# GpSimd's bias additions, the value projection's banks and the first scores moved; second biases gathered by expert number

## The reference

```python
x = x + gnn(layernorm(x), gW1, gb1, gW2, gb2)        # two graph convolutions over 10000 edges + self loops
# ffn of layernorm(x), 625 rows of 768:
h = ln(x, ln1_g, ln1_b); q, k, v = h @ Wq, h @ Wk, h @ Wv          # 12 heads of 64
x = x + softmax(causal(q k^T) * 768**-0.5) v @ Wp + bp
h2 = ln(x, ln2_g, ln2_b)
w, sel = top_k(h2 @ Wg, 1); w = softmax(w)           # one of 8 experts for each row
y = relu(h2 @ W1[e] + b1[e]) @ W2[e] + b2[e]         # 768 -> 3072 -> 768, for the chosen expert e
out = x_in + x + w * y                               # the outer residual too
```

## Time and profile before

| | us |
|---|---|
| median of 3 runs | 882.34 |
| lowest, highest | 880.31, 886.64 |
| the profiled execution: time | 882.35 |
| the profiled execution: span | 880.8 |
| busy in it: PE, DVE, ACT, POOL | 846.6, 713.1, 552.9, 78.3 |
| share of the clock granted to TensorE over the span | 0.993 |

### The profile page before, as it was taken

How to read it: one execution, slowest core, us unless ns; L and a number is a source line. 1 busy time by engine, 2 the same in 40 slices (tenths; PEclk the granted TensorE clock), 3 DMA queues, 4 the chain that set the end, 5 groups by cost and what they waited for, 6 DMA issues and landing times.

```text
span 880.8 us, 14635 instructions
## 1 busy us (share of the span) xinstructions
PE 846.6 (96%) x5326; PEld 815.4 (93%) x5326; DVE 713.1 (81%) x1102; ACT 552.9 (63%) x785; POOL 78.3 (9%) x85
## 2 busy tenths in 40 slices
PE   7999999989899998999989999999999999999997
PEld 7989999989789888898989999999999999999996
DVE  6999586873578787755788897998989899898996
ACT  4612341352577777614577877888878888787880
POOL 2000000230400000031600000000000000000041
PEclk9999999999999999999999999999999999999998
DMA  7030017162930033430799999999999999999984
GB/s 219 22 108 1 19 25 156 53 161 67 319 116 2 1 108 92 159 89 1 251 361 355 355 338 377 346 364 373 351 377 359 364 373 351 376 347 374 373 279 139
DMA packets 116232, 196.00 MB, mean 223 GB/s; under 512 B 34052, under 2 KB 83420, under 8 KB 116182
## 3 DMA queue, kind: packets, MB, share of 16 engines
q1 hardware_dynamic: 107858, 168.88, 56.4%
q0 software_dynamic: 6368, 24.19, 8.0%
q10 hardware_dynamic: 1956, 2.26, 1.0%
HBM read 177.40 MB, written 17.90 MB: 222 GB/s over the span
## 4 chain that ended last, share of the span: by engine, by line
PE 61%; DVE 19%; DMA 11%; issue 4%; ACT 4%; SPq 0%; DVEq 0%; ACTq 0%
PE ps L1502 12%; PE ps L1905 11%; DMA raw<-in_L_ffn_W 11%; PE ps L1924 10%; DVE wlo L1002 10%; PE ps L1686 7%; PE ps L1531 4%; PE ps L1757 3%; PE ps L1735 2%; PE ps L1582 2%; PE ps L1608 2%; PE ps L1720 2%; PE ps L1890 2%; ACT whi L668 2%; DVE ohs L1054 1%
## 5 line engine op out<-in xcount | busy, mean ns | idle before, releaser
L1002 DVE TENSOR_TENSOR wlo<-raw,whi 128x2304 fp32r<-128x2304 f32 (+1 forms) x150 | 352.7, 2359 | 22.8 <-ACT whi L668 22.4
L668 ACT ACTIVATE whi<-raw 128x2304 fp32r<-128x2304 f32 (+1 forms) x152 | 300.7, 1980 | 80.9 <-DMA raw<-in_L_ffn_W 33.7
L1924 PE MATMUL ps<-whi,hTT 128*128 128x384 f32 x768 | 201.5, 339 | 0.7 <-ACT oh7T L668 0.7
L1924 PEld LDWEIGHTS ps<-whi,hTT 128*128 128x128 f32 x768 | 139.1, 188 | 1.0 <-ACT oh7T L668 1.0
L1905 PE MATMUL ps<-whi,hgh 128*128 128x384 f32 x384 | 133.0, 346 | 1.0 <-DVE hgl L1002 1.0
L1924 PE MATMUL ps<-wlo,hTT 128*128 128x384 f32 x384 | 129.0, 336 | 0.0
L1905 PE MATMUL ps<-whi,hgl 128*128 128x384 f32 x384 | 129.0, 336 | 0.0
L1905 PE MATMUL ps<-wlo,hgh 128*128 128x384 f32 x384 | 128.4, 334 | 0.0
L1905 PEld LDWEIGHTS ps<-whi,hgh 128*128 128x128 f32 x384 | 72.2, 188 | 1.2 <-DVE hgl L1002 1.2
L1924 PEld LDWEIGHTS ps<-wlo,hTT 128*128 128x128 f32 x384 | 72.3, 188 | 0.0
L1905 PEld LDWEIGHTS ps<-wlo,hgh 128*128 128x128 f32 x384 | 72.3, 188 | 0.0
(11 more groups left out here) (294 smaller groups left out, 1589.2 us busy)
## 6 DMA issues: line engine op xcount, KB each, us to landing
raw<-in_L_ffn_W SPq DMA_DIRECT2D x128, 1152.0 KB, 6.9
hs_d<-bc POOLq DMA_DIRECT2D x13, 384.0 KB, 6.4
raw<-in_L_gnn_W SPq DMA_DIRECT2D x4, 1152.0 KB, 5.8
hs<-hs_d POOLq DMA_DIRECT2D x8, 384.0 KB, 5.6
ys_d<-ysb POOLq DMA_DIRECT2D x7, 384.0 KB, 5.9
raw<-in_L_ffn_Wv SPq DMA_DIRECT2D x6, 384.0 KB, 5.2
raw<-in_L_ffn_Wq SPq DMA_DIRECT2D x12, 192.0 KB, 3.6
raw<-in_L_ffn_Wk SPq DMA_DIRECT2D x12, 192.0 KB, 3.5
```

The source lines that it names most:

```text
L668: act.activation(out_, in_, func).then_inc(s, 1)
L1002: dve.tensor_tensor(out_, in_, hi_, ALU.subtract).then_inc(s, 1)
L1924: ins = mm(ps[0:CAP, 4 + half, 0:HB], l, rr, start=k == 0 and j == 0 and jj == 0, stop=k == FCH - 1 and j == JW - 1 and jj == 2)
```

## The change

It has seven parts.

1. **Graph part.** `P1_BANK` goes from (6, 0, 2, 6, 4) to (6, 6, 2, 6, 4), and `transform(1)` waits for `h0_out(0)` (s_hev 1) in place of all three `counts`; `transform(3)` waits for s_hev 2.
2. **Bias additions on POOL.** The third addition waits for the low part of Wv's second half (s_flo 6), the fourth and fifth for hTl chunks 2 and 4 (s_hTl).
3. **Value projection.** Its banks are 6 - 2(c%2) in place of 4 + 2(c%2); chunk 0 waits for four of the five `s_x1`, chunk 1 for the fifth.
4. **First scores.** The order of the first products is g = 0, 2, 1, then `scores(0)`, then g = 3; g = 1 goes to bank 6. ACT and DVE follow (`qk_out(3)` behind the first exponents and maxima).
5. **First weight chunk.** `split_hi(0, 0)` and `split_lo(0, 0)` are made in two halves; DVE's first half stands ahead of its wait for the gates, the second where the whole stood.
6. **Pick.** CHOICE_BUSY goes from 12 to 9, blocks lie in banks 6, 7, 5 by pairs (`picked`), and ACT starts on each of the first two pairs when it is there.
7. **Second biases.** oh8T, its five transposes, b2's hi and lo and all `bias_y` products go. Instead POOL, behind the first `next_in`, gathers b2's rows by `eidx` into `x2` (five indirect DMAs), and DVE adds them times wtok to `base` in steps 9 to 13 of the first tile. Y_BACK_AT goes from 10 to 8, and the fifth `others_y` moves ahead of the low parts of y.

```diff
 LAST_BANK = (0, 2, 6, 4, 0)
+QK_FIRST = (0, 2, 1, 3)
 FIN_ORDER = ((0, 0), (1, 0), (2, 0), (0, 1), (1, 1), (2, 1), (3, 0), (3, 1), (4, 0), (4, 1))
-Y_BACK_AT = 10
+Y_BACK_AT = 8
+B2_AT = 9
 OVER_N2 = 5
...
 FIRST_COUNTS_AT = 67
-P1_BANK = (6, 0, 2, 6, 4)
+P1_BANK = (6, 6, 2, 6, 4)
 PR = P + 2
...
 SHORT = 2
-TURN_BUSY, GATE_BUSY, RANK_BUSY, CHOICE_BUSY = 3, 3, 8, 12
+TURN_BUSY, GATE_BUSY, RANK_BUSY, CHOICE_BUSY = 3, 3, 8, 9
 EARLY = 4
...
+
+        def picked(m):
+
+            return ps[0:128, (6, 7, 5)[m // 2], m % 2 * 128:m % 2 * 128 + CAP]
...
-            return ps[:, 6 if g >= 4 else g, 0:HALF]
+            return ps[:, g if g in (0, 2, 3) else 6, 0:HALF]
...
+
+        def qk_count(g):
+
+            return C + (QK_FIRST.index(g) if g < 4 else g) + 1
...
                 g.wait_ge(s_n1, c + 1)
+                if c == 2:
+                    g.wait_ge(*split(2 * WV + 2))
+                elif c >= 3:
+                    g.wait_ge(s_hTl, 2 * c - 4)
                 gp.tensor_tensor(xf[:, c, :], xf[:, c, :], bc[1][0:P, :], ALU.add).then_inc(s_xfb, 1)
...
                 g.dma_start(tok(xf_d)[r0:r1, :, :], xf[r0:r1, :, :]).then_inc(s_xfst, 16)
-            g.dma_start(bc[1][0:E, :], b2[:, :]).then_inc(s_b2in, 16)
...
             next_in(0)
+            g.wait_ge(s_base, C)
+            for c in range(C):
+                g.indirect_dma_start(out=x2[:, c, :], out_offset=None, in_=b2[:, :],
+                                     in_offset=bass.IndirectOffsetOnAxis(ap=eidx[:, c:c + 1], axis=0)
+                                     ).then_inc(s_b2in, 16)
             with g.Fori(1, E) as t:
...
                 y_out(t)
-            g.wait_ge(s_base, C)
+            g.wait_ge(s_b2, C)
             g.wait_ge(s_route, 1)
...
                 if held:
-                    a.wait_ge(s_pj, C + 2 * held[-1] + 2)
+                    a.wait_ge(s_pj, C + max(2 * held[-1] + 2, 4))
                 else:
...
-                a.wait_ge(s_pj, C + g + 1)
+                a.wait_ge(s_pj, qk_count(g))
                 if not g:
...
             a.wait_ge(s_x2, C)
-            split_hi(0, 0)
+            a.wait_ge(s_raw[0], FULL[0] + 16)
+            act.activation(whi[0][:, 0:CH // 2], raw[0][:, 0:CH // 2], ACT.Copy).then_inc(s_mhalf, 1)
+            hi(whi[0][:, CH // 2:CH], raw[0][:, CH // 2:CH], s_mhi)
...
             step(dve.tensor_tensor(shift_, down(mv2[:, :, 0]), across(gbias[:, E:2 * E]), ALU.mult))
+            d.wait_ge(s_mhalf, 1)
+            dve.tensor_tensor(wlo[0][:, 0:CH // 2], raw[0][:, 0:CH // 2], whi[0][:, 0:CH // 2], ALU.subtract)
             d.wait_ge(s_gate, 1)
...
             dve.tensor_tensor(wtok[:, :], rt[:, 7, 0:C], rt[:, 7, 8:8 + C], ALU.mult)
-            split_lo(0, 0)
+            d.wait_ge(s_mhi, 1)
+            lo(wlo[0][:, CH // 2:CH], raw[0][:, CH // 2:CH], whi[0][:, CH // 2:CH], s_mlo)
             d.wait_ge(s_rank, 1)
...
                         lo(hTT_part(1, k - 2), bia[:, k % 2, :, :], hTT_part(0, k - 2), s_hTl2, relu=True)
+                    if first and B2_AT <= k < B2_AT + C:
+                        c = k - B2_AT
+                        d.wait_ge(s_b2in, 16 * C)
+                        d.wait_ge(s_base, C)
+                        dve.scalar_tensor_tensor(base[:, c, :], x2[:, c, :], wtok[:, c:c + 1], base[:, c, :],
+                                                 ALU.mult, ALU.add).then_inc(s_b2, 1)
                     if k == max(TILE_STEPS) + 1:
...
                 tile(t, t)
-            d.wait_ge(s_b2h, 1)
-            lo(b2l, bc[1][0:E, :], b2h, s_b2l)
-            d.wait_ge(s_base, C)
+            d.wait_ge(s_b2, C)
...
-            for c in range(C - 1):
+            for c in range(C):
                 others_y(c)
...
                 lo(wlo[0][0:CAP, part], ps[0:CAP, 4 + half, 0:HB], whi[0][0:CAP, part], s_yl)
-            others_y(C - 1)
             d.wait_ge(s_yin, C)
...
+            pe.wait_ge(s_hev, 1)
+            transform(1)
             pe.wait_ge(s_cint, len(GROUPS))
-            transform(1)
             pe.wait_ge(s_rows, 64)
...
             ins.then_inc(s_deg, 1)
-            pe.wait_ge(s_hev, 1)
+            pe.wait_ge(s_hev, 2)
             transform(3)
             pe.wait_ge(s_big, 1)
-            pe.wait_ge(s_hev, 2)
             mm(ps[0:1, 0, 0:2], big[:, 0:1], onesb[:, 0:2], start=True, stop=True).then_inc(s_bigs, 1)
...
                     turn_n1(c - 2)
-            pe.wait_ge(s_x1, C)
+            pe.wait_ge(s_x1, C - 1)
             pe.wait_ge(*split(2 * WV + 1))
...
                 pe.wait_ge(s_hTl, c + 1)
+                if c == 1:
+                    pe.wait_ge(s_x1, C)
                 if c >= 2:
                     pe.wait_ge(s_pjl, c - 1)
-                rows_product(hT, 2 * WV, c, 4 + 2 * (c % 2), None if c else {DC // 2: split(2 * WV + 2)}
+                rows_product(hT, 2 * WV, c, 6 - 2 * (c % 2), None if c else {DC // 2: split(2 * WV + 2)}
                              ).then_inc(s_pj, 1)
...
                 pe.wait_ge(s_ulo, unit_count(g // 2))
-                if g >= 4:
+                if g == 1:
+                    pe.wait_ge(s_pjl, C)
+                elif g == 4:
+                    pe.wait_ge(s_pjl, qk_count(1))
+                elif g > 4:
                     pe.wait_ge(s_pjl, C + g)
...
-            for g in range(4):
-                if g == 3:
-                    pe.wait_ge(s_gbr, 1)
+            for g in QK_FIRST[:3]:
                 qk_products(g)
...
                 n = score_cols(2 * t)
-                if c == 0:
+                if t == 0:
+                    pe.wait_ge(s_pjl, qk_count(2))
+                elif t == 1:
+                    pe.wait_ge(s_pjl, qk_count(3))
+                elif c == 0:
                     pe.wait_ge(s_pjl, C + 4 * (m + 1))
...
             scores(0)
+            pe.wait_ge(s_gbr, 1)
+            qk_products(3)
             next_pair(-1)
...
                 for c in range(C):
-                    ins = mm(blocks(6, 128, DC, CAP)[:, m, :], n2[:, c, m * 128:(m + 1) * 128], oh0[:, c, :],
+                    ins = mm(picked(m), n2[:, c, m * 128:(m + 1) * 128], oh0[:, c, :],
                              start=c == 0, stop=c == C - 1)
-                if m == EARLY - 1:
+                if m % 2 and m < EARLY:
                     ins.then_inc(s_pick, 1)
...
                 for c in range(C):
-                    nc.tensor.transpose(blocks(6, 128, C, P)[:, c, :], oh0[:, c, :], ident[0:P, 0:P])
-                for c in range(C):
-                    ins = nc.tensor.transpose(blocks(4, E, C, P)[:, c, :], rt[:, 3, c * E:(c + 1) * E], ident[0:P, 0:P])
+                    ins = nc.tensor.transpose(blocks(6, 128, C, P)[:, c, :], oh0[:, c, :], ident[0:P, 0:P])
                 ins.then_inc(s_ohT, 1)
...
-            def bias_y(c, half):
-                for i, t in enumerate((b2h, b2l)):
-                    mm(ps[0:P, LAST_BANK[c] + half, 0:HB], oh8T[0:E, c, :], t[:, half * HB:(half + 1) * HB],
-                       start=i == 0, stop=False)
-
...
                     ins = mm(ps[0:P, LAST_BANK[c] + half, 0:HB], oh7T[:, c, :], t[0:CAP, half * HB:(half + 1) * HB],
-                             start=False, stop=i == 1)
+                             start=i == 0, stop=i == 1)
                 return ins
-            pe.wait_ge(s_b2l, 1)
             pe.wait_ge(s_hga, DC * (E + 1) - EARLY)
             for half in range(2):
-                for c in range(3):
-                    bias_y(c, half)
                 pe.wait_ge(s_yl, half + 1)
```

More of the change, by code:

```diff
@@ L211, in build @@
                     [("n2", [P, C, D], F32), ("h2T", [128, DC, NP], F32)],
-                    [("oh7T", [128, C, P], F32R), ("oh8T", [128, C, P], F32R),
-                     ("r3pad", [128, RB - 2 * C * P - 2 * DF // 128 * CAP], F32),
+                    [("oh7T", [128, C, P], F32R),
+                     ("r3pad", [128, RB - C * P - 2 * DF // 128 * CAP], F32),
                      ("hTT", [128, FCH, 2, JW, CAP], F32R)])
@@ L241, in build @@
         rt, tp, iotac, oh0 = R2["rt"], R1["tp"], R2["iotac"], R1["oh0"]
-        oh7T, oh8T, hTT = R3["oh7T"], R3["oh8T"], R3["hTT"]
+        oh7T, hTT = R3["oh7T"], R3["hTT"]
         def hTT_part(i, n):
             return hTT[:, FCH - 1 - n, i, :, :]
-        b2h, b2l = whi[1][0:E, 0:D], wlo[1][0:E, 0:D]
         ps = ctx.enter_context(nc.psum_tensor("ps", [128, 8, 512], F32))
@@ L391, in build @@
         s_used, s_mhi, s_mlo = (sem(n) for n in ("chunks_used", "expert_hi", "expert_lo"))
+        s_mhalf = sem("first_expert_half_hi")
         s_hidev, s_hidT, s_bia, s_hTh2, s_hTl2 = (sem(n) for n in (
@@ L818, in _ @@
             unit_hi(3)
+            qk_out(2)
+            unit_hi(5)
             qk_out(1)
-            unit_hi(5)
-            qk_out(2)
-            qk_out(3)
             def wp_hi(k):
@@ L872, in _ @@
                 if i == 0:
+                    qk_out(3)
                     qk_out(4)
@@ L921, in tile_hi @@
```

(20 more changed lines are left out.)

9 lines of the change are left out of this document (3 added, 6 removed).

## The result

The changed kernel takes 894.3 us (median of 4 runs, 890.8 to 896.8) where the kernel before took 882.0 beside it: ratio 1.013, 95% interval 1.010 to 1.017. It is slower, by some 12 us; 876.8 was predicted, and 882.5 was the upper end of the range. The profiled execution took 893.8 us (span 892.3).

The account below looks back on a forecast made before the run. Weights' arrival was taken to bound the first three expert tiles, PE those from the fourth, earlier stages in series; -1.5 - 2.25 - 1.0 - 1.25 - 3.55 + 4.0 = -5.55 against 882.35 gave 876.8 us, range 871 to 882.5.

Parts of the forecast that it names:

- chunks 9 to 11 land later and hold ACT's `hid`: 1.5 us of PE: First tile: the added gather delays these weight chunks, costing PE 1.5 us in front of chunk 8.
- the part on the first tile: Second biases in the first tile: gather beside the weights and DVE's wait for it, taken as +4.0 us.
- My upper bound, 7: First tile: the gather's cost is 7 us if all three losses add up; the lower bound was 0.5.
- The wait on DVE: First tile: DVE, at 467.8 behind low part 11, stands 1.3 to 3.8 us for the gathered biases.
- the later of my two cases: First tile: last gathered rows land at 471.6, 10.5 us after the fifth issue, as in the scatter; the earlier was 469.1.
- Rival 3: First tile: slow gather issues on POOL, 6.77 us each, make DVE stand 20 us; +11.5, 893.9 us; chance 0.04.
- rival 1: First tile: the gather is hidden and costs 0.5, the change is -9.05, 873.3 us; chance 0.23.
- The tail, -3.55: Behind the last expert product: without `bias_y` DVE becomes the bound and its ten additions end at 873.1, not 876.78.
- an earlier gather of y costs 0: Last tile: issuing this gather at 8 for 10 costs 0, the last chunks' low parts being some 4 us ahead.
- rival 2: Value projection: POOL's third addition only moves the collision with DVE; -1.5 in place of -2.25, 877.6 us; chance 0.13.
- the forecast 6.0: Front stages together: the first expert product comes 6 us earlier, at 422.7.
- Gains ahead of 429 us count in full: Stages before the experts: time gained there moves the DMA stream forward too, if nothing loads it anew.

Follow-up runs that it names:

- experiment 6: Parts 1 to 6 alone plus the gather of biases at the changed kernel's place, read by nobody: 888.2 us, 1.007 of the kernel before.
- experiment 7: Changed kernel with the gather replaced by five plain copies of the same size, rows of x, on the same queue: 890.2 us, 1.010 of the kernel before.
- experiment 5: Changed kernel with DVE's five additions of the second biases moved behind the first tile, gather kept in place: 896.5 us, 1.016 of the kernel before.
- e3: Changed kernel with the gather reading 625 different rows of hs_d by slot instead of b2 by expert number: 894.1 us, 1.014 of the kernel before.
- e4: Changed kernel with Y_BACK_AT back at 10, so a later gather of the experts' outputs: 890.6 us, 1.010 of the kernel before.
- Experiment 4: Changed kernel without the gather of biases, DVE's five additions kept, adding what x2 holds: 879.6 us, 0.999 of the kernel before.
- e5: The kernel of Experiment 4: changed kernel without the gather of biases, five additions kept: 879.6 us, 0.999 of the kernel before.
- e2: Kernel before with only part 7, the second biases, changed: 898.7 us, 1.019 of the kernel before.
- e11: The kernel of experiment 6: parts 1 to 6 alone plus a gather of biases that nobody reads: 888.2 us, 1.007 of the kernel before.
- e1: Changed kernel with the second biases as before, so parts 1 to 6 alone: 878.2 us, 0.995 of the kernel before.
- e8: e1 with ACT copying the hidden values ahead of its weight split in the first tile: 879.1 us, 0.996 of the kernel before.

## Why the prediction was wrong

The span came out 17.0 us longer than -5.55 makes it. Tiles 1 and 2 are 10.7 of that (14.7 for 4.0), the tail 4.55, the last tile 2.4, and the front part gave 0.6 more than forecast.

**The step that failed** is the sentence "chunks 9 to 11 land later and hold ACT's `hid`: 1.5 us of PE" in the part on the first tile. The mechanism was right, but for PE standing ahead of chunk 9 and not 8; the size was 8.1 us over two tiles (experiment 6). I had reckoned 1.97 MB (five times 375 KB are 1.92) at 356 GB/s, 5.5 us, and then let the weights' lead hide most of it, though the earlier trace rows had the DMA 0.99 busy in that tile with nothing to make it up from. Two things came on top: the rate fell to 268 GB/s while both queues had work, and each of the long stalls cost 1.7 us more through the clock. My upper bound, 7 for both the contention and the wait, was too near for the same reason.

The Trainium skill (DMA: Bandwidth & Descriptors, queues, rings and completion order) says that a DMA engine takes turns between the queues that have work, a packet at a time. By that rule a gather, once issued, takes its share ahead of weights asked for long before it. The rows agree: 56.5% and 46.8% of the engines' time for the two queues in experiment 7.

**The wait on DVE.** The prediction gives 469.1 to 471.6 for the last landing and 467.8 for DVE's turn. These are times of the kernel before with only the 1.27 us of the pick taken off, so the other 4.75 us of the forecast lead have to come off before they are set beside the trace of after: 464.4 to 466.9, and 463.1. Measured are 473.95 and 467.55. The fifth issue began at 454.2, where I had 456.4 in this clock, since the issues were quicker than my 3.05 us apiece; but it was in flight for 19.7 us where I had taken the scatter's 10.5. So the rows landed 7 us later than the later of my two cases, and DVE came 4.5 later itself, behind stalls that I hadn't forecast. What is left is a wait of 6.43 for 3.8. The errors don't cancel: that 473.95 looks near to 471.6 comes from the two clocks. With the additions it costs 4.4 us in tile 1 (experiment 5), in place of 2.5, and how long DVE waits is uneven: 2.36 us in e3, 0.84 in e4. Rival 3 gave 893.9, which is the time measured, but by issues of 6.77 us each; these did not come (maximum 3.34), so it was right by number only. Experiment 4 shows what rival 1 would have brought at best: 879.6, not 873.3, as the tail's gain wasn't there either.

**The tail, -3.55: the failed step on this side.** DVE is the bound as predicted and the ten additions run back to back, but they begin later and what follows is longer:

```profile
874.16 4.73 DVE L1478 SCALAR_TENSOR_TENSOR base<-x,wtok,base 125x768 f32<-125x768 f32 x5
...
880.20 5.67 DVE L1491 SCALAR_TENSOR_TENSOR base<-ps,wtok,base 125x384 f32<-125x384 f32 x10 [0.38 <-PE ps L1973]
```

From the last expert product (876.70) to the last addition (885.87) are 9.2 us, not 6.8, against 10.5 before. (The prediction's own 873.1 for 876.78 is a gain of 3.7, not 3.55.) All five `others_y` stand between the late low part 127 and the split of y; before, the first three ran from 862.01 on, while PE still multiplied. And from the last addition to the end of the span are 6.4 us where they were 4.0: ten additions in 5.67 us hand over the five output chunks faster than the DMA writes them (its engines are 0.7 to 0.9 busy from 883.2 to 889.6), so what DVE gained the stores kept. e5 shows the same without any gather of biases (5.8 us, tail 15.3). Only where the last chunk came so late that `others_y` were done ahead of it is the tail short (e2: 6.55 us from product to addition, 12.7 in all), and then the last tile had paid for it (60.8 us). That an earlier gather of y costs 0 was wrong as well: +2.4 in the last tile.

**What held.** Graph part -1.35 (predicted -1.5). Value projection -1.48 (predicted -2.25): rival 2 happened and gave its own number (-1.5), though the collision was over at 177.96 and not at 179.6. DVE's `var` step took 1.77 us beside POOL's third addition, in place of 0.17, and ended as the addition did. The Trainium skill (GPSIMD Engine Reference, specifications) names two SBUF inputs or a 2-port mode as what collides; this step has one input, so the row speaks for the wider reading. First scores -1.12 (-1.0), first chunk and pick -1.16 (-1.25). These four are 0.9 short of the forecast 6.0. They were made good by 1.5 us that I had not forecast: near 350 us the kernel before fell to the lower clock level (granted 0.83 over 345 to 355) and the changed one stayed at 1.00. The edits alone don't account for that: both profiles without them fell there (before, e2), but of the eleven with them two fell as well (e3 and e11, near 345). The sum at the first expert product was thus right partly by luck; without it the lead would be some 5.1. "Gains ahead of 429 us count in full" was not right: of e1's 6.15 us some 4 reach the end (2.6 to 6.0 by its interval).

## What to carry to other kernels

Where a stage is bound by a stream of weights, cost a new transfer beside it by its whole time at the rate of two queues together (here some 270 GB/s, not 356), add the clock after each long stall, and ask which engine stands in its queue for the late chunk and what is behind it; a lead of 4 us in front of PE hides none of 8. Put such a transfer where the DMA rests, even ahead of more urgent ones: the same gather before the scatter cost 10 us less. And a shorter chain of additions at the end is worth only what the output stores let through. Of the versions that compute the right thing, parts 1 to 6 alone are the one to keep: 0.995 of the time before (0.993 to 0.997). e8 is equal to it, and no other has its interval below 1.
